# Local transformer of an eight-stage kernel: VectorE adds the mask, GpSimd subtracts the row maximum, TensorE's mask products go

## The reference

```python
q = l2norm(q) * qs; k = l2norm(k) * ksc            # then rotary embedding
mask = (it < jb) | (it > jb + w) | (jb == -1)
sim = jnp.einsum('bhwie,bhwje->bhwij', bq, bk2) * QK_SCALE
sim = jnp.where(mask, -jnp.finfo(sim.dtype).max, sim)
attn = jax.nn.softmax(sim, -1)
out = jnp.einsum('bhwij,bhwje->bhwie', attn, bv2)
```

## Time and profile before

| | |
|---|---|
| median of 3 runs | 6369.78 us (6368.16 to 6382.02) |
| the profiled execution's own time | 6383.19 us |
| its span, first to last instruction | 6381.5 us |
| PE / PEld / DVE / ACT / POOL busy in the span | 84% / 55% / 68% / 52% / 41% |
| mean granted TensorE clock | 0.917 |

### The profile page before, as it was taken

The page is one execution under the profiler, slowest core; times in us unless marked ns, Lnnn a source line. Parts: engine busy times, 40 slices in busy tenths (PEclk is TensorE's granted clock), DMA queues, the critical chain, the costliest instruction groups (busy, mean ns, idle before and its releaser), DMA issues. The chain is left out here.

```text
span 6381.5 us, 131778 instructions
## 1 busy us (share of the span) xinstructions
PE 5339.7 (84%) x50817; PEld 3481.6 (55%) x50817; DVE 4357.1 (68%) x7060; ACT 3348.6 (52%) x5697; POOL 2611.2 (41%) x1601
## 2 busy tenths in 40 slices
PE   6999655996888888888888889898888887996866
PEld 3455222553666666666665666566666664662233
DVE  4887796774777677777776777677777774773222
ACT  3555322554666566656665665566665564552123
POOL 2555210001555455555554555455555552660000
PEclk8999766997999999999999999999999998996857
DMA  2111000000000100000001000100010000000000
GB/s 59 62 53 53 17 0 6 2 2 25 11 10 10 28 11 10 12 26 13 10 10 29 10 10 10 29 10 10 10 29 11 11 11 12 2 2 7 13 0 17
DMA packets 74175, 105.07 MB, mean 16 GB/s; under 512 B 21576, under 2 KB 52504, under 8 KB 71072
## 3 DMA queue, kind: packets, MB, share of 16 engines
q1 hardware_dynamic: 65648, 101.28, 5.7%
q10 hardware_dynamic: 8256, 0.03, 0.1%
HBM read 61.19 MB, written 2.36 MB: 10 GB/s over the span
## 5 line engine op out<-in xcount | busy, mean ns | idle before, releaser
L2147 POOL TENSOR_TENSOR lt_qk<-lt_qk,lt_rot 128x1024 f32<-128x1024 f32 x384 | 904.9, 2357 | 525.0 <-DVE lt_rot L2501 525.0
L2157 POOL TENSOR_TENSOR lt_prob<-lt_prob,lt_total 128x1024 f32<-128x1024 f32 x192 | 365.2, 1902 | 1239.2 <-DVE lt_total L2527 1218.4
L2196 PE MATMUL lt_ps<-lt_w_qk,lt_xs 128*128 128x512 f32 x1536 | 759.1, 617 | 54.9 <-issue 33.2
L2152 POOL TENSOR_TENSOR lt_qk<-lt_qk,lt_rnorm 128x1024 f32<-128x1024 f32 x384 | 727.7, 1907 | 57.8 <-ACT lt_rnorm L2375 50.2
L2247 PE MATMUL lt_ps<-lt_z,lt_fold 128*128 128x256 f32 x3072 | 678.8, 379 | 1.1 <-ACT lt_z L2403 1.1
L2247 PEld LDWEIGHTS lt_ps<-lt_z,lt_fold 128*128 128x128 f32 x3072 | 583.6, 190 | 121.7 <-ACT lt_z L2403 24.5
L2368 ACT ACTIVATE lt_sq<-lt_ps 128x1024 f32<-128x1024 f32 x384 | 393.4, 1024 | 481.3 <-PE lt_ps L2196 473.1
L2498 DVE TENSOR_TENSOR lt_qk<-lt_ps,lt_table 128x1024 f32<-128x1024 f32 x384 | 466.2, 1214 | 154.9 <-ACT lt_sq L2368 150.7
L2501 DVE TENSOR_TENSOR lt_rot<-lt_ps,lt_table 128x512 f32<-128x512 f32 x768 | 489.1, 676 | 0.0
L2508 DVE TENSOR_REDUCE lt_norm<-lt_sq 128x16 f32<-128x1024 f32 x384 | 464.0, 1208 | 2.2 <-ACT lt_log L2372 0.6
L2196 PEld LDWEIGHTS lt_ps<-lt_w_qk,lt_xs 128*128 128x128 f32 x1536 | 272.0, 193 | 319.1 <-issue 278.1
(11 more groups left out here) (438 smaller groups left out, 10657.8 us busy)
## 6 DMA issues: line engine op xcount, KB each, us to landing
mb_bs<-mb_rows SPq DMA_DIRECT2D x16, 1536.0 KB, 7.7
lt_xw<-lt_xw SPq DMA_DIRECT2D x192, 128.0 KB
mb_bs<-mb_rows SPq DMA_DIRECT2D x16, 512.0 KB, 4.3
lt_xs<-h SPq DMA_DIRECT2D x96, 64.0 KB, 1.9
lt_w_qk<-in_L_ffn_Wqkv SPq DMA_DIRECT2D x6, 1024.0 KB, 5.1
lt_xs<-h SPq DMA_DIRECT2D x96, 63.8 KB, 2.0
lt_wvT<-in_L_wvT SPq DMA_DIRECT2D x6, 512.0 KB, 7.1
lt_wo<-in_L_ffn_Wo SPq DMA_DIRECT2D x6, 512.0 KB, 8.3
```

The source lines that it names most:

```text
L2147: pool.tensor_tensor(qk[:, u, :, :], qk[:, u, :, :], rot[:, u % 2, :, :], ALU.add).then_inc(sg["added"], 1)
L2152: pool.tensor_tensor(qk[:, u, :, :], qk[:, u, :, :], rnorm[:, u, :, :].to_broadcast([P, H, DH]), ALU.mult).then_inc(sg["qk"], 1)
L2196: last = pe.matmul(AT[u][:, 512 * k:512 * k + 512], xs[:, m.j, c:c + P], w_qk[:, a, 512 * k:512 * k + 512], start=True, stop=True)
```

## The change

VectorE's first step of the softmax becomes scores plus mask, out of PSUM into `prob` (it signals `s_read`); its second is the maximum over `prob`, out of SBUF. GpSimd gets a new step `shifted`, `prob` minus the maximum, in place, behind `unit_length` of the last unit for half 0 and behind `normalize` of half 0 for half 1. ScalarE's exponential waits for `shifted`. TensorE's two mask products per half go; the first small product into each bank starts the accumulation instead, and a semaphore increment of TensorE stands in front of the products. GpSimd's copies of identity and mask at the start of the stage go.

```diff
-        mask = sb("mask", [P, 2, H // 2, 2 * WIN], BF16)
-        identb = sb("identb", [P, P], BF16)
...
@@ gpsimd
-            pool.wait_ge(sg["c_in"], 32)
-            pool.tensor_copy(identb[:, :], core.ident[:, :]).then_inc(sg["zeros"], 1)
-            for t in range(2):
-                pool.tensor_copy(mask[:, t, :, :], maskf[:, t, :, :].to_broadcast([P, H // 2, 2 * WIN])).then_inc(sg["zeros"], 1)
-            for name, each in (("added", 4), ("qk", 4), ("prob", 2)):
+            for name, each in (("added", 4), ("qk", 4), ("shifted", 2), ("prob", 2)):
...
+            def shifted(m, t):
+                pool.wait_ge(sg["max"], 2 * m.n + t + 1)
+                pool.tensor_tensor(prob[:, t, :, :], prob[:, t, :, :], nmax[:, t, :, :].to_broadcast([P, H, 2 * WIN]),
+                                   ALU.subtract).then_inc(sg["shifted"], 1)
...
                     unit_length(front, 3)
+                    shifted(front, 0)
                     normalize(front, 0)
+                    shifted(front, 1)
@@ tensor
             def scores(m, t, to):
                 pe.wait_ge(sg["qkT"], 4 * m.n + 2 * t + 2)
-                for k in range(2):
-                    pe.matmul(to[:, 512 * k:512 * k + 512], identb[:, :], mask[:, t, :, :].rearrange("p h c -> p (h c)"),
-                              start=True, stop=False, skip_group_check=True)
+                pe.sem_inc(sg["score_step"], 1)
                 for g in range(H // 2):
...
-                                             start=False, stop=(g == H // 2 - 1), skip_group_check=True, tile_position=(r, WIN * w))
+                                             start=(g == 0), stop=(g == H // 2 - 1), skip_group_check=True, tile_position=(r, WIN * w))
@@ scalar
             def exps(m, t):
-                act.wait_ge(sg["s_read"], 2 * m.n + t + 1)
+                act.wait_ge(sg["shifted"], 2 * m.n + t + 1)
@@ vector
             def softmax(m, t, src):
                 s = src.rearrange("p (h c) -> p h c", h=H)
                 dve.wait_ge(sg["scores"], 16 * m.n + 8 * t + 8)
-                nc.vector.tensor_reduce(nmax[:, t, :, 0], s, AX.X, ALU.max).then_inc(sg["max"], 1)
-                dve.wait_ge(sg["max"], 2 * m.n + t + 1)
                 dve.wait_ge(sg["p_turned"], 2 * m.n + t - 1)
-                nc.vector.tensor_tensor(prob[:, t, :, :], s, nmax[:, t, :, :].to_broadcast([P, H, 2 * WIN]), ALU.subtract).then_inc(sg["s_read"], 1)
+                nc.vector.tensor_tensor(prob[:, t, :, :], s, maskf[:, t, :, :].to_broadcast([P, H, 2 * WIN]), ALU.add).then_inc(sg["s_read"], 1)
+                dve.wait_ge(sg["s_read"], 2 * m.n + t + 1)
+                dve.wait_ge(sg["shifted"], 2 * m.n + t - 1)
+                nc.vector.tensor_reduce(nmax[:, t, :, 0], prob[:, t, :, :], AX.X, ALU.max).then_inc(sg["max"], 1)
```

More of the change, by code:

```diff
@@ L2112, in next_layer @@
                     sp.sem_inc(sg["xw_moved"], 32 * AHEAD)
-                    sp.wait_ge(sg["zeros"], 6)
+                    sp.wait_ge(sg["zeros"], 3)
                     sp.wait_ge(sg["h"], B // 2)
@@ L2182, in _ @@
             pe.wait_ge(sg["ln_log"], B // 2)
-            pe.wait_ge(sg["zeros"], 6)
+            pe.wait_ge(sg["zeros"], 3)
             def project(m, u):
@@ L2362, in _ @@
             ln.act(act)
-            act.wait_ge(sg["zeros"], 6)
+            act.wait_ge(sg["zeros"], 3)
             def square(m, u):
```

## The result

| | before | after |
|---|---|---|
| median, both on one chip (4 runs each) | 6373.44 us | 6435.57 us (6426.21 to 6441.73) |
| the profiled execution's own time | 6383.19 us | 6440.16 us |
| its span | 6381.5 us | 6438.4 us |
| mean granted TensorE clock | 0.917 | 0.913 |

The ratio is 1.0095 [1.0076, 1.0114]: slower by 62 us where 58 were forecast. The sum was made on profiled executions: 57 us between them, with 61.9 us more between the first and the last `attended` of the local transformer and 5 us less elsewhere.

What follows compares the result with a forecast made beforehand. TensorE, 88% busy, nearly bounds the kernel; a chain through scores, `xn`, `up` 0 and `hidden` sets the rest. 95 x 0.44 = 42 us plus 16 for the clock: 58 us slower, 6428 on the median; range 6372 to 6480.

Steps and rivals of the forecast that it cites:

- Mask products: TensorE, before the scores of each half: removing the mask products takes 0.53 us off the chain per half.
- The step: TensorE's semaphore increment before the scores: 0.05 us for half 0, nothing for half 1, bounds 0 and 0.28.
- Add and maximum: VectorE's two softmax passes: add 1.22 us like the old subtraction, maximum from SBUF equal to PSUM's (1217 against 1224 ns).
- The rule on PSUM and SBUF sources: VectorE's maximum: a 62-cycle difference in fixed time, estimated 0.06 us each, would make the sum 12 us better; not adopted.
- The hold-up: GpSimd's half 0 subtraction keeps VectorE's L2545 waiting until 0.14 us after it ends; `xn` and `up` 0 0.97 us later.
- The first rival: L2545 is not held up by GpSimd: `xn` 0.48 us earlier, 44 us faster, 6326; chance 0.14.
- the second: L2545 starts before GpSimd is ready: `xn` 0.48 us earlier, the add 0.08 later, 8 us, 6378; chance 0.10.
- What stayed covered: Half 0's exponential, sum and reciprocal 0.66 us later, covered by 0.83; `hidden` not held up by GpSimd's second subtraction.
- The clock: TensorE's longer pause before `up` 0 brings more low-clock stretches: one more in three items, 32 x 0.5 = 16 us.
- 2.15 for half 0: Expected duration in us of GpSimd's `shifted` for half 0 in the changed profile, against 1.90 for half 1.

Runs made afterwards that it cites:

- e1: The kernel before with its mask products removed and nothing in their place, so the mask is left out of the computation; 6301.01 us, ratio 0.9879.
- e4: The changed kernel with GpSimd's subtraction as two instructions of eight heads each; 6347.05 us, ratio 0.9953.
- e5: The changed kernel with four idle 128x256 products in TensorE's pause for `xn`, before `up` 0; 6436.02 us, ratio 1.0079.
- e3: The changed kernel with GpSimd's subtraction of half 0 kept back until `xn` is done; 6467.68 us, ratio 1.0139.
- e11: The changed kernel with GpSimd's subtraction in two instructions and `turn_x` with its copy moved earlier; 6358.72 us, ratio 0.9965.
- e2: The kernel before, mask products kept, but VectorE takes the maximum from PSUM and copies scores to `prob`, and GpSimd subtracts; 6587.85 us, ratio 1.0325.
- e7: e3 with five idle 128x256 products before `turn_p` of half 0, behind the wait for the GELU; 6489.83 us, ratio 1.0164.
- e8: The kernel before with only `turn_x` and its copy moved earlier, `turn_x` into TensorE's pause before `mean`; 6349.07 us, ratio 0.9949.
- e9: The changed kernel with eight TensorE semaphore increments before the scores instead of one; 6631.02 us, single run.
- e6: The kernel before with `turn_x` moved into TensorE's pause before `mean`, half 1's mask products into that before `up` 0; 6319.63 us, ratio 0.9894.
- e10: e3 with two idle 128x512 products right behind `up` 1, ahead of the wait for the GELU; 6397.38 us, ratio 1.0023.

## Why the prediction was right, step by step

- **Mask products.** Forecast 0.53 per half; e1 has 0.47 and 0.52 per segment, the former with the semaphore step in it. The step, taken as 0.05, was 0.06 by e1's mean. In the one item shown the scores start 0.15 after the k copy's end (2959.81 against 2959.66), where the mask products of an item before started 0.06 after it, which puts the step at 0.09. Both are within the bounds.
- **Add and maximum.** The add takes 1224 ns and the maximum out of SBUF 1.22, as taken. The rule on PSUM and SBUF sources that the prediction weighed and put aside (the Trainium skill, "VectorE: DVE Perf Modes", "The TRN2 errata — SBUF-src ops pay a fixed extra latency per instruction") would have made the maximum shorter by an estimated 0.06; the groups have 1220 ns out of SBUF against 1224 out of PSUM, so it isn't there.
- **The hold-up.** Each link was right: GpSimd gets through when L2543 ends and not before, ends 1.76 after it (forecast 1.90 - 0.14), and L2545 ends 0.15 after GpSimd (forecast 0.14; 0.15 is also the median of 95 items). The Trainium skill ("SBUF — State Buffer", "Who interferes with whom") has it as a lock held for a whole instruction; e4 agrees, with 1.01 us for L2545 when GpSimd's instruction is cut in two. The first rival ("no hold-up") fell with 1.87 us at the median of 96, the second ("VectorE gets in first") with GpSimd's issue 0.25 us before L2543's end.
- **What stayed covered.** The later exponential cost nothing: VectorE still idled 0.95 between the reciprocal and the add of half 1 (forecast 0.83), and L2553 ran its usual 1.25 beside GpSimd.
- **The clock.** 32 more low items at 0.5 were forecast; it was 20 more at about 0.75. The product, 16 us, came out by luck, two errors that cancel. The place, behind the pause before `up` 0, holds for 17 low stretches, which e5 makes go; the rest of the increase lies around `mean`. That filling the pause gives the 16 us back isn't shown: e5's time fell by too little, and its low items are longer.
- **Small misses.** The 5 us of the layer steps weren't in the sum. And "2.15 for half 0" in the list of what would show it was wrong by my own term: 0.25 of waiting and 1.90 - 0.14 make 2.01, which is what the row has.

Where the forecasts of the experiments failed, it was mostly the clock term. I took it as a small addition to the chain. In e3 and e11 it decided the order of the kernels, and in e2 it was 77 us where 15 were expected. Other steps failed too: in e4 the full-clock item was 0.17 shorter than forecast, in e7 the products were put on the path, in e8 the chain became 0.24 shorter for a reason that stays open, and in e9 an increment cost 0.15 instead of 0.09.

## What to carry to other kernels

An instruction handed to GpSimd to relieve VectorE can hold VectorE up for its whole length, as here L2545 with both its operands in SBUF (1.87 us for 0.41), while instructions that read PSUM ran on beside it; before moving such a step, look up what VectorE issues next, and if it must be there, cut the GpSimd instruction in pieces (a ratio of 0.9953 for 1.0095 here, for one loop). And price every pause of TensorE by the products behind it as well as by itself: moving existing work into pauses (e6, 1.1% faster than before) was worth nearly as much as leaving the mask products out altogether (e1, 1.2%).

## What the runs showed that I had not expected

- A kernel can get faster by useless work: e10's two products keep TensorE busy 1.9 us more per item (181.6 us over 95) and take the ratio from 1.0139 to 1.0023, and the low items from 72 to 26.
- The length of a pause alone doesn't tell. Before `mean`, 131.3 us of idle time (1.4 per item) has a low stretch behind it in 23 items; before `up` 0 in e8, 137.7 us have none, but 189.5 and 205.9 have (e11 and the changed kernel, `up` at 424 and 416 ns).
- A semaphore increment in TensorE's queue cost about 0.15 us in a row of eight, with the array waiting (e9, one run); a single one cost 0.06 to 0.09. Behind other products, before half 1's, even eight cost nothing at the median.
- The segment from `xn` to `ffn_out` became 0.24 us shorter by moving `turn_x`, which lies ahead of it (e8). Why is open.

Not tried: L2545 in another form or on another engine, which would take the hold-up away without touching GpSimd, and e6 together with e4.
